# A recommendation network on one core: gated weight loads, a last tile in quarters, results turned by VectorE, and the rows of one field fetched by SyncE

## What is computed

```python
lin = bias + x_num @ w_num + lin_cat[fid, x_cat].sum(axis=1)
vn = x_num[:, :, None] * v_num[None, :, :]
vc = v_cat[fid, x_cat]
v = jnp.concatenate([vn, vc], axis=1)
sum_v = v.sum(axis=1)
interactions = 0.5 * (sum_v * sum_v - (v * v).sum(axis=1)).sum(axis=1, keepdims=True)
deep_in = jnp.concatenate([x_num, vc.reshape(vc.shape[0], -1)], axis=1)
h = jax.nn.relu(deep_in @ W1 + b1)      # 1024 wide
h = jax.nn.relu(h @ W2 + b2)            # 512 wide
h = jax.nn.relu(h @ W3 + b3)            # 256 wide
return lin + interactions + (h @ Wo + bo)
```

## Time and profile before

| | us |
|---|---|
| median of 3 runs | 155.88 |
| lowest and highest run | 154.91 and 156.05 |
| the profiled execution | 154.75 |
| its span, first to last instruction | 153.0 |

### The profile page before, as it was taken

One profiled execution on the slowest core, in us unless ns is written; L12 is line 12 of the kernel. 1 busy time (PEld: TensorE's weight loads), 2 busy tenths in 40 slices (PEclk: granted clock), 3 DMA queues, 4 the chain that ended last, 5 costly groups with the idle time before them and its releaser, 6 DMA issues.

```text
span 153.0 us, 2072 instructions
## 1 busy us (share of the span) xinstructions
PE 135.2 (88%) x661; PEld 105.0 (69%) x661; DVE 77.7 (51%) x216; ACT 58.0 (38%) x153; POOL 99.6 (65%) x111
## 2 busy tenths in 40 slices
PE   0303999879999999999999999999999999999994
PEld 0102776547776676888767878778787887776992
DVE  4310587997699687232435524333446223353712
ACT  4501578666376631142333132223431423234120
POOL 3777777777777777777777777777777777700000
PEclk9999999999999999999999999999999999999999
DMA  4999677987777643343234343431344433310000
GB/s 107 372 123 311 103 208 197 298 261 198 192 232 201 175 27 29 28 29 25 27 25 33 26 26 28 27 31 27 25 30 27 30 28 25 28 9 4 0 0 0
DMA packets 6750, 13.66 MB, mean 89 GB/s; under 512 B 2578, under 2 KB 2708, under 8 KB 6740
## 3 DMA queue, kind: packets, MB, share of 16 engines
q0 software_dynamic: 3328, 3.47, 25.6%
q1 hardware_dynamic: 3412, 10.07, 21.0%
HBM read 13.53 MB, written 0.00 MB: 88 GB/s over the span
## 4 chain that ended last, share of the span: by engine, by line
PE 67%; DVE 13%; DMA 12%; issue 3%; ACT 2%; POOL 1%; DVEq 0%
PE acc L593 12%; PE acc L590 12%; PE acc L583 11%; DMA raw<-in_weights 6%; DMA g<-in_table,rows 6%; DVE w_lo L371 4%; PE acc L659 4%; PE acc L655 3%; PE acc L656 3%; PE xt_ps L574 3%; PE acc L677 2%; DVE num_r L376 1%; ACT w_hi L234 1%; DVE hidden L412 1%; PE ht_ps L566 1%
## 5 line engine op out<-in xcount | busy, mean ns | idle before, releaser
L225 POOL DMA_INDIRECT g<-in_table,rows x104 | 98.8, 950 | 33.2 <-issue 28.3
L398 DVE TENSOR_TENSOR x_lo<-xt_ps,x_hi 128x128 fp32r<-128x128 f32 x52 | 15.0, 288 | 50.0 <-ACT x_hi L241 50.0
L241 ACT ACTIVATE x_hi<-xt_ps 128x128 fp32r<-128x128 f32 x52 | 14.3, 275 | 68.6 <-PE xt_ps L574 68.4
L590 PE MATMUL acc<-w_lo,x_hi 128*128 128x512 f32 x96 | 34.8, 443 | 0.0
L583 PE MATMUL acc<-w_hi,x_hi 128*128 128x512 f32 x96 | 31.1, 405 | 0.8 <-ACT x_hi L241 0.5
L593 PE MATMUL acc<-w_hi,x_lo 128*128 128x512 f32 x96 | 30.8, 402 | 1.0 <-DVE x_lo L398 1.0
L593 PEld LDWEIGHTS acc<-w_hi,x_lo 128*128 128x128 f32 x96 | 18.1, 191 | 6.0 <-DVE x_lo L398 1.8
L583 PEld LDWEIGHTS acc<-w_hi,x_hi 128*128 128x128 f32 x96 | 17.7, 191 | 5.4 <-ACT x_hi L241 1.4
L234 ACT ACTIVATE w_hi<-raw 128x1024 fp32r<-128x1024 f32 x18 | 19.0, 1055 | 6.2 <-DMA raw<-in_weights 6.1
L574 PE MATMUL xt_ps<-ident,g 128*128 128x128 f32 x52 | 14.4, 278 | 6.8 <-DMA g<-in_table,rows 6.8
L590 PEld LDWEIGHTS acc<-w_lo,x_hi 128*128 128x128 f32 x96 | 14.7, 193 | 4.9 <-issue 0.9
(11 more groups left out here) (99 smaller groups left out, 154.4 us busy)
## 6 DMA issues: line engine op xcount, KB each, us to landing
raw<-in_weights SPq DMA_DIRECT2D x18, 512.0 KB, 4.7
g<-in_table,rows POOLq DMA_INDIRECT x104, 3.4
hidden<-in_numeric SPq DMA_DIRECT2D x4, 108.1 KB, 7.0
consts<-in_row_consts SPq DMA_DIRECT2D x1, 129.0 KB, 9.2
cat<-in_x_cat SPq DMA_DIRECT2D x1, 39.0 KB, 4.3
cat<-in_x_cat SPq DMA_DIRECT2D x1, 13.0 KB, 1.7
out<-raw SPq DMA_DIRECT2D x1, 1.5 KB
out<-raw SPq DMA_DIRECT2D x1, 0.5 KB
```

The source lines that it names most:

```text
L225: pool.indirect_dma_start(g[:, c, a * ROW:(a + 1) * ROW], None, table, bass.IndirectOffsetOnAxis(rows[:, t, 2 * c + a:2 * c + a + 1], 0))\
L241: act.activation(x_hi[:, n % SLOTS, :], xt(n), ACT.Copy).then_inc(xhi_done, 1)
L398: dve.tensor_tensor(x_lo[:, n % SLOTS, :], xt(n), x_hi[:, n % SLOTS, :].bitcast(F32), ALU.subtract).then_inc(xlo_done, 1)
L590: pe.matmul(acc[:, :], x_hi[:, n % SLOTS, :], w_lo[:, c, w], start=False, stop=False)
```

## The change

Five edits. (1) Loads are gated and reordered on SP: behind w0 and w1, SP waits until chunk 0 of the first tile has landed, then issues the other categories and w2; w3 waits for chunk 1, w4 for chunk 2; the numeric inputs move behind w5 and w6, the constants behind w7. VectorE computes the first row numbers ahead of its memset, and the other ones inside the first tile's loop; numeric work moves to later chunks of the first tile. (2) The last tile's hidden layer is rectified, turned and split in quarters, with the matmuls of W2 between the turns. (3) `result_row` is gone from TensorE: VectorE adds `deep` and `fm` into a column and transposes it in blocks of 32 x 32. (4) The 128 rows of one field (field 23, the second of chunk 11) of the last tile are fetched by 128 transfers of one row each, issued by SP with the row number in a register; registers are filled 32 at a time from SBUF; five such transfers stand behind each of w8 to w17, the other 78 behind w17. They go into an additional buffer of `g`, with nothing to wait for, so POOL issues 103 gathers. (5) The rings `x_hi` and `x_lo` have three slots instead of four, which makes room for it.

```diff
-SLOTS = 4
+SLOTS = 3
+LATE = 1
+LATE_CHUNK = CHUNKS - 2
+LATE0 = 2 * LATE_CHUNK + 2 - LATE
...
+        quarter_ps = [ht_ps[0], ht_ps[1], xt_ps[1], acc1[0]]
...
         def chunk_landed(eng, t, c):
-            eng.wait_ge(rows_in[c], 32 * (t + 1))
+            if is_late(t, c):
+                eng.wait_ge(late_in, 16 * LATE * P)
+                if LATE == 1:
+                    eng.wait_ge(late_pool_in, 16)
+            else:
+                eng.wait_ge(rows_in[c], 32 * (t + 1))
...
             sp.dma_start(cat[:, 0, :], x_cat[0:P, :]).then_inc(cat_in[0], 16)
             weight(0)
             weight(1)
+            chunk_landed(sp, 0, 0)
             sp.dma_start(cat[:, 1:TILES, :], by_tile[:, 1:TILES, :]).then_inc(cat_in[1], 16)
+            sp.dma_start(late_row[:, :], late_cat).then_inc(late_cat_in, 16)
             weight(2)
+            chunk_landed(sp, 0, 1)
+            weight(3)
+            chunk_landed(sp, 0, 2)
+            weight(4)
+            weight(5)
             sp.wait_ge(num_zeroed, 1)
-            for k in range(P // STACK):
-                sp.dma_start(hidden[k * STACK:k * STACK + NROWS, :], numeric).then_inc(num_in, 16)
-            weight(3)
+            numeric_stacks(0, 2)
+            weight(6)
+            numeric_stacks(2, 4)
+            weight(7)
             sp.dma_start(consts[:, :], row_consts).then_inc(consts_in, 16)
-            for i in range(RING, ITEMS):
+            numbers = [sp.alloc_register(f"late_number{i}") for i in range(STACK)]
+            def late_rows(first, end):
+                for n in range(first, min(end, LATE * P)):
+                    if n % STACK == 0:
+                        sp.load(numbers, late_row[0:1, n:n + STACK])
+                    a, p = 2 - LATE + n // P, n % P
+                    sp.dma_start(g[p:p + 1, CHUNKS, a * ROW:(a + 1) * ROW],
+                                 table[bass.ds(sp.snap(numbers[n % STACK]), 1), :]).then_inc(late_in, 16)
+            sp.wait_ge(late_ready, LATE)
+            for i in range(8, ITEMS):
                 weight(i)
...
+                late_rows(5 * (i - 8), 5 * (i - 7))
+            late_rows(5 * (ITEMS - 8), LATE * P)
+            by_block = out.rearrange("(t b i) o -> t b (i o)", t=TILES, i=STACK)
+            sp.wait_ge(result_turned, 1)
+            for t in range(LAST):
+                sp.dma_start(by_block[t], turned[t:P:STACK, 0, :]).then_inc(stored, 16)
+            sp.wait_ge(result_turned, 2)
+            sp.dma_start(by_block[LAST], turned[LAST:P:STACK, 1, :]).then_inc(stored, 16)
...
-                    for a in range(2):
+                    for a in range(2 - LATE if late else 2):
                         pool.indirect_dma_start(
...
+            act.wait_ge(l1_half0, TILES)
+            for q in range(2):
+                act.activation(h1[:, quarter(q)], acc1[0][:, quarter(q)], ACT.Relu).then_inc(relu1a, 1)
+            for q in range(4):
+                act.wait_ge(h1t_done, 2 * LAST + q + 1)
+                act.activation(h1t_hi[:, 2 * q:2 * q + 2, :], quarter_ps[q][:, 0:QUARTER], ACT.Copy)\
+                   .then_inc(h1hi_done, 1)
...
+            def add_result(t):
+                dve.wait_ge(deep_done, t + 1)
+                dve.wait_ge(fm_done, t + 1)
+                dve.tensor_tensor(result[:, t:t + 1], deep[:, t:t + 1], fm[:, t:t + 1], ALU.add)\
+                   .then_inc(result_done, 1)
+            def turn_results(a):
+                dve.wait_ge(result_done, LAST + a)
+                dve.transpose(turned[:, a, :], result[:, :]).then_inc(result_turned, 1)
...
-            def result_row(t, n):
-                pe.wait_ge(fm_done, t + 1)
-                pe.matmul(xt_rows(n), fm[:, t:t + 1], ident[:, :], start=True, stop=False)
-                pe.wait_ge(deep_done, t + 1)
-                pe.matmul(xt_rows(n), deep[:, t:t + 1], ident[:, :], start=False, stop=True)\
-                    .then_inc(row_turned, 1)
...
+            pe.wait_ge(relu1a, TILES)
+            turn_quarter(0)
+            pe.wait_ge(relu1a, TILES + 1)
+            turn_quarter(1)
+            pe.wait_ge(relu1b, TILES)
+            turn_quarter(2)
             pe.wait_ge(h1hi_done, 2 * LAST + 1)
             for acc, at in parts:
-                part2_high(range(0, 4), acc, at)
+                part2_high(range(0, 2), acc, at)
+            pe.wait_ge(relu1b, TILES + 1)
+            turn_quarter(3)
+            pe.wait_ge(h1hi_done, 2 * LAST + 2)
+            for acc, at in parts:
+                part2_high(range(2, 4), acc, at)
```

More of the change, by code:

```diff
@@ L38, with deepfm_kernel @@
 RING = 4
-SLOTS = 4
+SLOTS = 3
+LATE = 1
+LATE_CHUNK = CHUNKS - 2
+LATE0 = 2 * LATE_CHUNK + 2 - LATE
 def chunks_of(j):
     return 2 * j, min(2 * j + 2, CHUNKS)
-def deepfm_kernel(nc, x_cat, table, numeric, row_consts, weights, out):
+def deepfm_kernel(nc, x_cat, late_cat, table, numeric, row_consts, weights, out):
     with ExitStack() as ctx:
@@ L91, in deepfm_kernel @@
         deep = sb("deep", [P, TILES])
+        result = sb("result", [P, STACK])
+        turned = sb("turned", [P, 2, STACK])
         hidden = sb("hidden", [P, NCOLS])
@@ L155, in deepfm_kernel, with quarter, is_late, slot_of @@
         block = ctx.enter_context(nc.Block())
+        def quarter(q):
+            return slice(q * QUARTER, (q + 1) * QUARTER)
         def xt(n):
             return xt_ps[n % 2][:, 0:P]
[L160 to L173 removed]
+        def is_late(t, c):
+            return t == LAST and c == LATE_CHUNK
+        def slot_of(t, c):
+            return CHUNKS if is_late(t, c) else c
+        def slots_of(t, j):
+            c0, c1 = chunks_of(j)
+            return slice(c0, slot_of(t, c1 - 1) + 1, max(1, slot_of(t, c1 - 1) - c0))
+        def embeddings(t, j):
+            return g[:, slots_of(t, j), 1:1 + 2 * K]
+        def linear(t, j):
+            return g[:, slots_of(t, j), 0:2 * ROW:2 * ROW - 1]
+        def chunk_landed(eng, t, c):
+            if is_late(t, c):
[4 more added lines that the diff above has]
+                eng.wait_ge(rows_in[c], 32 * (t + 1))
         @block.sync
@@ L183, in weight, with numeric_stacks @@
                 sp.dma_start(raw[:, i % RING, :], weights[i]).then_inc(raw_in[i % RING], 16)
+            def numeric_stacks(k0, k1):
+                for k in range(k0, k1):
+                    sp.dma_start(hidden[k * STACK:k * STACK + NROWS, :], numeric).then_inc(num_in, 16)
             sp.dma_start(cat[:, 0, :], x_cat[0:P, :]).then_inc(cat_in[0], 16)
@@ L217, in _ @@
                 for c in range(CHUNKS):
-                    if t > 0:
+                    late = is_late(t, c)
+                    if t > 0 and not late:
                         pool.wait_ge(xt_done, (t - 1) * CHUNKS + c + 1)
@@ L366, in row_numbers, with late_row_numbers @@
                                          ALU.min, ALU.add).then_inc(rows_ready, 1)
+            def late_row_numbers():
+                dve.wait_ge(late_cat_in, 16)
+                dve.tensor_scalar(late_wrap, late_row[:, :], 0.0, float(VOCAB), ALU.is_lt, ALU.mult)\
+                   .then_inc(late_step, 1)
+                dve.wait_ge(late_step, 1)
+                dve.scalar_tensor_tensor(late_wrap, late_row[:, :], -float(VOCAB), late_wrap,
+                                         ALU.max, ALU.add).then_inc(late_step, 1)
+                dve.wait_ge(late_step, 2)
+                for a in range(LATE):
+                    cols = slice(a * P, (a + 1) * P)
+                    dve.tensor_scalar(late_row[:, cols], late_wrap[:, cols], float(VOCAB - 1),
+                                      float((LATE0 + a) * VOCAB), ALU.min, ALU.add).then_inc(late_ready, 1)
             def low_part(d):
@@ L536, in _ @@
                         sums(t, c // 2)
-            hidden1_relu(LAST)
-            hidden1_low(LAST, 0)
-            hidden1_low(LAST, 1)
+            dve.wait_ge(l1_done, TILES * CHUNKS)
+            for q in range(2, 4):
+                dve.tensor_scalar(h1[:, quarter(q)], acc1[1][:, quarter(q - 2)], 0.0, None, ALU.max)\
+                   .then_inc(relu1b, 1)
+            for q in range(4):
+                dve.wait_ge(h1hi_done, 2 * LAST + q + 1)
+                dve.tensor_tensor(h1t_lo[:, 2 * q:2 * q + 2, :],
+                                  quarter_ps[q][:, 0:QUARTER].rearrange("p (c b) -> p c b", b=P),
+                                  h1t_hi[:, 2 * q:2 * q + 2, :].bitcast(F32), ALU.subtract)\
+                   .then_inc(h1lo_done, 1)
             interactions(LAST)
@@ L767, in _ @@
                 step(t, 5)
-                step(t, 6)
-                layer1_a(t, 7)
-                turn_rows(t, 8)
-                pe.wait_ge(xlo_done, t * CHUNKS + 8)
-                result_row(t - 1, t * CHUNKS + 7)
-                layer1_b(t, 7)
-                pe.wait_ge(result_done, t)
-                for c in range(8, CHUNKS - 1):
+                for c in range(6, CHUNKS - 1):
                     step(t, c)
                 layer1_last(t)
-            turn_hidden1(LAST)
```

(5 more changed lines are left out.)

90 lines of the change are left out of this document (44 added, 46 removed).

## The result

The changed kernel is slower: 158.11 us, median of 4 runs (156.68 to 158.5), against 155.45 us (154.91 to 156.05) for the kernel before in the same comparison, a ratio of 1.018 with an interval of 1.013 to 1.023. I had forecast 152.4 us, faster. The profiled execution took 158.5 us, its span 156.7.

What follows compares the result with a forecast made beforehand. TensorE was busiest, with POOL's gather stream only 1.4 us behind being the bound and next to limit. Gains of 2.65 + 0.5 + 0.38 = 3.53 us gave 151.2 profiled, 152.4 us as median; range 151.0 to 159.0.

Steps and rivals of the forecast that it cites:

- Part 1: Opening and first tile: gated loads bring chunk 0 at 8.4 instead of 14.1 us and win 2.5 us at w8.
- Part 2: SP's queue, w8 to w17: one-row issues of 0.47 us, register fills of 0.8; w17 goes at 46.9 us.
- Part 3: Result rows off TensorE: three steps save 2.16 us; at the very end 0.38 us, between 0 and 0.62.
- Part 4: Last tile's hidden layer in quarters: layer 2's first matmul 0.75 us earlier, gain 0.5 us, between 0.2 and 0.8.
- Part 5: POOL, last tile: one gather less, last landing at 135.0 us, last chunk turned 2.65 us earlier than 137.65.
- the limit of POOL: Last tile: the last gather stops TensorE's gain, landing at 136.2 us with all 104 gathers, 135.0 with one less.
- first rival: SP's queue: its issue rate becomes the bound and the kernel slower, 158.9 us at 0.65 an issue; chance 0.16 above 0.62.
- fourth rival: SP's register fills: at 6.1 us each, two fills delay w17 by 10.6 us, giving 161.4 us; chance 0.08.
- The third: Opening: gates hold weights too long or an issue costs 0.51 to 0.55 us; TensorE stays the bound, 153.1 us; chance 0.12.

Runs made afterwards that it cites:

- the two openings above: Kernels without gates, late rows behind w17, numeric work at its old chunks: memset behind the row numbers, chunk 0 turned at 11.69 us; memset in front, 14.45 us.
- The small copies: Changed kernel with each numeric copy moving 16 of 1730 columns, all instructions, gates and rows kept: 154.27 us, ratio 0.996 to the kernel before.
- the trial that was to tell: Changed kernel without gates, rows behind w17, VectorE's numeric low parts one chunk later (after chunks 8 and 9): 158.17 us, ratio 1.013 to the kernel before.
- the pair above: Changed kernel without gates, rows behind w17, numeric work at its old chunks: 152.72 us (0.989); also memset first and row numbers up front: 153.0 us (0.990).

## Why the prediction was wrong

**The step that failed** is Part 1's "beside weights a gather takes 4.5 us", together with "Numeric work is moved, not removed: no gain". I priced the move of the numeric work by what is done, not by what it lies beside, and put its transfers at nothing. Before, the copies ran in the 9.23 us of the earlier trace rows in which TensorE waited for rows anyway: they had a cover. They, or the loads that move with them, lengthened that wait, by the two openings above, but 2.8 us less of it brought only 0.3. The gates let the rows in ahead and put the copies among w5 to w7, into the running tile. There a gather landed in 11.12 us, TensorE waited 3.93 us for it and ran the next chunks at the lower clock, and most of the loss stays to the end because the order from there on is fixed. The small copies show it: 3.3 us by the ratios. The early start of 5.9 us brings nothing that can be seen, since the weights behind it came later; at chunk 4 it was already down to 1.0. w8 went at 22.44 us, not 21.2, a win of 1.3 for 2.5: the sixth gather opened the gate of w4 at 15.01 us where I had 14.3, and VectorE worked out the row numbers of the late field ahead of w4's low part, from 20.40 to 21.10.

**The half of Part 1 on the engines** is worth 1.6 us by the medians, 1.8 by the ratios: numeric work begun at chunk 7 (1.000) against chunk 4 (0.989), nothing else changed, without gates and with the rows behind. Whether that is the lost distance between producer and consumer, or the place among the late weights, stays open: the trial that was to tell made a second wait of the same kind. It shows only how dear a wait of 4 us in that stretch is: 158.17 against 154.34, with a granted clock of 0.80 from 34 to 60 us. Open too is whether the gates cost or bring anything by themselves in a kernel that computes all; no run had them without a fault beside them. That three slots cost nothing was not tried by itself either; the kernels of the pair above have three slots and took 152.7 and 153.0 us, near the 152.4 forecast without a price for them.

**Part 2** had the row right and the fill wrong. One-row issues start 0.42 us apart (48.37, 48.79), inside my bounds and below the 0.505 that the forecast could stand. A fill takes 2.13 us, not 0.8, and nothing was there to hide it: w9 goes 4.74 us behind w8, where I had 2.68 + 0.8. Seven intervals of 2.5 to 2.9 us and the two of 4.7 with a fill in them make w8 to w17 27.4 us (22.70 to 50.07 with small copies) for my 25.7 and the 23.6 of the earlier trace rows. With w8 itself 1.5 us late in that run, w17 goes 3.2 us behind my 46.9. By the rule of the Trainium skill's page "Runtime: NRT & Kernel Launch" ("Instruction fetch mechanics", about 200 ns for each register) it would have been 6.4 us; the trace has 2.12 / 32, some 66 ns for each. The fill lay between my value and the page's. That page of the Trainium skill has loads from HBM in view; this one reads SBUF, so the trace need not contradict it.

**Part 3** held. The changed kernel is 5.98 us behind at the second tile's first transpose (53.15 for 47.17) and 3.85 behind at the last turn: from there on the steps without result rows gave 2.13 us for my 2.16. The end:

```profile
154.22 0.08 DVE L520 DVE_READ_ACCUMULATOR junk_h<-acc,consts 128x1 f32 x1
...
154.34 0.16 DVE L527 TENSOR_TENSOR result<-deep,fm 128x1 f32<-128x1 f32 x1
...
154.53 0.21 DVE L532 STREAM_TRANSPOSE turned<-result 128x32 f32<-128x32 f32 x1
154.77 0.50 SPq L258 DMA_DIRECT2D out<-turned  x1
```

The add took 0.16 and the transpose 0.21 us where I had 0.2 each, and from the start of the last accumulator read to the issue there are 0.55 us for 0.86 (151.47 - 150.61 in the earlier trace rows), a gain of 0.31 for my 0.38.

**Part 4** was over-priced, though inside its bounds of 0.2 to 0.8 us. Layer 2's first matmul starts at 145.03, 3.53 us after the last turn, where before there were 4.13 (141.78 - 137.65); I had 3.4. But of these 0.60 only 0.24 arrive at the end: from the last turn to the last issue it is 13.27 us for 13.82, 0.55 in all, of which the results have 0.31. My reading is that TensorE had work in between either way, which has to be done at some time; no run tried the quarters alone.

**Part 5 and the limit of POOL** were right in both forms, 135.09 and 136.22 us measured for 135.0 and 136.2. The change never came to them.

**The rivals.** The first had the sign, SP's issue rate, and not the cause: its issue is 0.42, and with the rows behind the weights the kernel is no faster. Its mechanism is real nonetheless, worth 1.9 us where the gates are off, and by the trace the fill of the fourth rival makes it: nine intervals of 2.5 us without fills are 22.5 us, less than the 23.6 of the earlier trace rows, and two fills add 4.2. The third, "the gates hold weights too long", was the nearest. I let it go no further than 2.35 us on the sixth gather; that gather was only 0.7 us late, and it was those issued from 15 to 21 us that cost the time, behind transfers that I had not priced at all. The sum by the runs: 152.4 as forecast, 1.9 for what stays with small copies (154.27 - 152.4), 3.8 for the copies (158.11 - 154.27). In the 1.9 lie SP's fills and pace, the moved work on the engines and the gates together. Taken away one after the other without gates, the first two are worth 1.9 and 1.6 us, 3.5 together (156.26 to 152.72). With gates and small copies both are in, and the kernel is only 1.6 us above 152.72. Either they overlap there or the gates bring something back; how they share it isn't settled. The measured 158.11 lies in the stated range only because of the room left for the first rival's issue rate, which didn't occur: that is luck.

## What to carry to other kernels

When an edit lets something urgent go first, list what it pushes back, and price each such transfer by what runs beside it at its new place: dead time at the start of a kernel is cover, and what lay there was nearly free. Before moving a producer later, look at the distance to its consumer on the other engine. And where two costs sit on the same queue, one hides the other in an experiment: take both away, then put each back alone.

## What the hardware showed that I had not expected

Four copies of 108 KB, 16 rows of 6,920 bytes each, cost far more than their 432 KB: in the stretch from 22.4 to 28.7 us the DMA share was 1.01 at 184 GB/s, where with small copies it was 0.85 at 242 GB/s. The low rate isn't theirs alone: in the kernel before the same copies lay beside weights and just as many gathers (eight from 5 to 14 us), and there the share of 1.05 went with 242 GB/s. Gathers were late there too, 6.4 to 9.2 us for those issued before 11 us. The gathers issued from 15 to 20 us landed, after and before (least, median, most):

```profile
DMA to landing us min/median/max: 6.9/9.7/11.1
```

```profile
DMA to landing us min/median/max: 3.7/4.2/4.5
```

With small copies only one of these five landings is on record, that of the gather issued at 14.9 us, ahead of the copies: 6.5 us, for 6.9 with the whole copies. Some of the delay thus comes from the weights that the gates bunch there. For the four gathers issued from 21 to 25 us all three kernels have it, after, with small copies, before:

```profile
DMA to landing us min/median/max: 7.0/7.9/8.9
```

```profile
DMA to landing us min/median/max: 3.6/4.6/5.7
```

```profile
DMA to landing us min/median/max: 5.0/5.2/5.8
```

There the copies account for all of the difference. A load of 32 of SP's registers takes 2.12 us, while issues from a register address follow each other in 0.42 us, no slower than plain ones in the opening (0.47). And an idle stretch is paid twice: the granted clock was 0.82 in the 6.3 us of waiting and 0.57 in the 5.3 us behind it. The granted clock doesn't show all of this. Behind the opening's wait in the kernel before, two matmuls took as long as behind this one, while the clock granted from 14 to 18 us stands at 1.00 (chain, before):

```profile
15.45 0.85 PE acc L583 x2
```
